# A gated mLSTM and mixture-of-experts block on one core: expert tiles written out, routing counts in a bank of their own, and warm-up matmuls in the routing waits

## What is computed

```python
def _L0_ffn_ref(hidden_states, w_gate, w1, w3, w2):
    E, TOPK, H, I = (8, 2, 256, 512)
    logits = SOFTCAP * jnp.tanh(x @ w_gate / SOFTCAP)      # 1024 tokens
    probs = jax.nn.softmax(logits, axis=-1)
    _, idx = jax.lax.top_k(probs, TOPK)
    weights = probs * one_hot(idx, E).sum(-2)
    for e in range(E):
        h = jax.nn.silu(x @ w1[e]) * (x @ w3[e])
        out = out + h @ w2[e] * weights[:, e:e + 1]
x = x + jnp.tanh(g_xattn[0]) * mlstm(_layernorm(x), ctx, ctx, ...)
x = x + jnp.tanh(g_ffn[0]) * _L0_ffn_ref(_layernorm(x), ...)
```

## Time and profile before

| | us |
|---|---|
| median of 3 runs | 223.19 (222.64 to 225.13) |
| profiled execution, its own time | 223.34 |
| its span, first to last instruction | 221.6 |

### The profile page before, as it was taken

The page is one execution under the profiler, slowest core; times in us unless marked ns, Lnnn a source line. Parts: engine busy times, 40 slices in busy tenths (PEclk is TensorE's granted clock), DMA queues, the critical chain, the costliest instruction groups (busy, mean ns, idle before and its releaser), DMA issues.

```text
span 221.6 us, 4536 instructions
## 1 busy us (share of the span) xinstructions
PE 194.2 (88%) x1327; PEld 139.9 (63%) x1328; DVE 159.6 (72%) x356; ACT 139.9 (63%) x281; POOL 92.1 (42%) x96
## 2 busy tenths in 40 slices
PE   8899899989889831779999999999999999999930
PEld 3378554444436621268888888888788888888720
DVE  6896764688989979998777857667666676767520
ACT  2487878898965697736666645565566665665510
POOL 8100254347470000611555556556445565642222
PEclk9999999999999885699999999999999999999997
DMA  4999999921010124120232233234333223343221
GB/s 111 313 366 376 372 374 373 372 77 47 3 47 3 57 77 151 47 53 24 47 50 47 47 50 49 47 49 70 50 55 59 51 47 47 47 57 37 27 24 24
DMA packets 20032, 23.41 MB, mean 106 GB/s; under 512 B 3888, under 2 KB 15152, under 8 KB 20016
## 3 DMA queue, kind: packets, MB, share of 16 engines
q1 hardware_dynamic: 13696, 16.94, 22.3%
q0 software_dynamic: 4464, 6.16, 17.2%
q10 hardware_dynamic: 1856, 0.10, 0.6%
HBM read 17.95 MB, written 5.24 MB: 105 GB/s over the span
## 4 chain that ended last, share of the span: by engine, by line
PE 72%; DVE 12%; ACT 5%; DMA 4%; issue 4%; POOL 1%; ACTq 0%; DVEq 0%; POOLq 0%
PE bank L1451 29%; PE bank L1266 7%; PE bank L1471 6%; PE bank L1483 5%; PE bank L1462 5%; PE bank L1306 3%; PE bank L1474 3%; DMA x_sb<-in_x_dram 3%; ACT arena L510 2%; PE bank L1433 2%; DMA out_dram<-hraw,sidx 2%; PE bank L1282 2%; PE bank L1337 1%; PE bank L1187 1%; DVE st L803 1%
## 5 line engine op out<-in xcount | busy, mean ns | idle before, releaser
L470 POOL DMA_INDIRECT out_dram<-hraw,sidx x23 | 37.6, 1633 | 52.5 <-DVE hraw L1140 32.8
L1451 PE MATMUL bank<-arena_r,xn_sb_r 128*128 x184 | 57.1, 391 | 0.0
L1451 PE MATMUL bank<-w_sb_r,xn_sb_r 128*128 x92 | 38.2, 415 | 1.5 <-DVE xn_sb_r L1084 1.2
L1451 PEld LDWEIGHTS bank<-arena_r,xn_sb_r 128*128 128x128 f32 x184 | 34.6, 188 | 7.0
L431 POOL TENSOR_SCALAR_AFFINE_SELECT arena<-arena 128x1024 f32<-128x1024 f32 x16 | 17.6, 1102 | 36.6 <-ACT arena L540 36.6
L674 ACT ACTIVATE x_sb<-bank 128x512 f32<-128x512 f32 x23 | 13.8, 599 | 28.6 <-PE bank L1451 28.6
L453 POOL DMA_INDIRECT cvT<-xnorm_scratch,gidx x12 | 13.8, 1146 | 32.1 <-DVE gidx L1038 24.2
L853 DVE TENSOR_TENSOR arena<-bank,arena 128x1024 f32<-128x1024 f32 x16 | 19.6, 1222 | 6.7 <-POOL arena L431 6.6
L1089 DVE TENSOR_TENSOR x_sb<-x_sb,bank 128x512 f32<-128x512 f32 x23 | 15.7, 684 | 9.0 <-ACT x_sb L674 8.9
L1451 PEld LDWEIGHTS bank<-w_sb_r,xn_sb_r 128*128 128x128 f32 x92 | 17.3, 188 | 5.0 <-issue 2.2
L975 DVE TENSOR_TENSOR w_sb_r<-w_sb,arena_r 128x512 fp32r<-128x512 f32 (+1 forms) x32 | 20.1, 684 | 0.1
(11 more groups left out here) (229 smaller groups left out, 389.6 us busy)
## 6 DMA issues: line engine op xcount, KB each, us to landing
w_sb<-in_L_ffn_w_dram SPq DMA_DIRECT2D x24, 512.0 KB, 9.2
x_sb<-in_x_dram SPq DMA_DIRECT2D x2, 512.0 KB, 6.7
arena<-in_ctx_dram SPq DMA_DIRECT2D x2, 512.0 KB, 9.4
out_dram<-x_sb SPq DMA_DIRECT2D x8, 128.0 KB, 1.8
xnorm_scratch<-xn_sb SPq DMA_DIRECT2D x8, 128.0 KB, 1.7
out_dram<-hraw,sidx POOLq DMA_INDIRECT x23, 3.8
cvT<-xnorm_scratch,gidx POOLq DMA_INDIRECT x12
hraw<-xnorm_scratch,gidx POOLq DMA_INDIRECT x11, 3.3
```

The costliest lines, as they stand in the source:

```text
L470: nc.gpsimd.indirect_dma_start(out=out[:, :], out_offset=bass.IndirectOffsetOnAxis(ap=sidx[:, i:i + 1], axis=0), in_=y_sb[i % 2], in_offse ...
L1451: last = nc.tensor.matmul(ps_scores[p][:, n, :], a, w, start=(k == 0 and j == 0), stop=(k == KC - 1 and j == 2))
```

## The change

- **Loops written out.** The `Fori` loops of ACT and DVE over the expert tiles become plain Python loops, with constant semaphore values and offsets. PE's loop stays. On DVE the load of a tile's expert moves from the start of a step to between `lower_w2` and `hidden` of the step before.
- **A third y buffer.** `y_sb` gets `zrow` as a third entry, and the wait on earlier scatters is one tile looser.
- **Counts.** PE makes the counts ahead of the ranks, in `ps_tr`, with a signal of their own (`s_cnt`); one more matmul with a constant adds 63.5. DVE rounds them up to whole tiles by a max and an add of 2^30 in float32, and the scan takes 2^30 off again, so `starts` holds slots. `ctile` and the reduction over it go.
- **slotf** is copied by ACT.
- **lower_weights(0, 2)** moves from before the wait for the ranks to behind `tabc`, beside parts 1 and 3.
- **Warm-ups.** 16 behind the last logits, 14 behind the ranks, 1 between the two groups of table matmuls, 15 for 8 behind the tables, 4 behind `turn_x(0)`.
- **The first gate-up** takes its 12 matmuls in another order: the 8 with the upper part of x first, waiting for `s_xh`; then the 4 with the lower part, waiting for `s_xts`.

```diff
@@ ACT
             act.wait_ge(s_slf, 1)
+            follow(nc.scalar.activation(slotf[:], sloti[:, 1, NS - LATE_OH:], ACT.Copy))
...
-            with act.Fori(1, E // 2) as pair:
...
+            for e in range(2, E):
+                for k in range(SPLIT):
+                    upper_weights(e, k)
+                store_hT(e - 2, e % 2)
+                silu(e - 1, (e - 1) % 2)
+                upper_x(e, e % 2)
...
-            with act.Fori(FAST, NT - 2, 2) as i:
...
+            for i in range(FAST, NT - 2):
+                upper_hT(i, i % 2)
+                upper_w2(i + 1, 1 - i % 2)
+                silu(i + 1, 1 - i % 2)
+                upper_x(i + 2, i % 2)
+                second_part(i)
@@ DVE, routing
-            lower_weights(0, 2)
+            dve.wait_ge(s_cnt, 1)
+            link(nc.vector.tensor_scalar(ntile[:, 1:], ps_tr[:, 0:E], P // 2 + 0.5, ROUND, ALU.max, ALU.add))
+            link(nc.vector.tensor_tensor_scan(starts[:], ntile[:], unround[:], 0.0, ALU.add, ALU.add))
+            base, eslot = starts[:, 0:E], starts[:, 1:]
+
             dve.wait_ge(s_rank, 1)
-            link(nc.vector.tensor_tensor(ctile[:], ps_small[:, 192:192 + E].unsqueeze(2).to_broadcast([P, E, E]),
-                                         iota_c[:, :].unsqueeze(1).to_broadcast([P, E, E]), ALU.is_gt))
-            link(nc.vector.tensor_reduce(ntile[:, 1:], ctile[:], AX_X, ALU.add))
-            link(nc.vector.tensor_tensor_scan(starts[:], ntile[:], zeros[:], 0.0, ALU.add, ALU.add))
...
+            link(nc.vector.tensor_tensor(slotm[:], base.unsqueeze(1).to_broadcast([P, B, E]),
+                                         ps_small[:, 128:128 + B * E].rearrange("p (b e) -> p b e", b=B), ALU.add))
...
-            nc.vector.tensor_scalar(sloti[:, 1, :], sloti[:, 0, :], P - 1, None, ALU.bitwise_and).then_inc(s_vch, 1)
-            chain[0] += 1
+            nc.vector.tensor_scalar(sloti[:, 1, :], sloti[:, 0, :], P - 1, None, ALU.bitwise_and).then_inc(s_slf, 1)
             link(nc.vector.tensor_scalar(sloti[:, 2, :], sloti[:, 0, :], 7, None, ALU.logical_shift_right))
-            nc.vector.tensor_copy(slotf[:], sloti[:, 1, NS - LATE_OH:]).then_inc(s_slf, 1)
...
-            lower_weights(0, 1)
-            lower_weights(0, 3)
+            for k in range(1, SPLIT):
+                lower_weights(0, k)
@@ DVE, tiles
-            def sum_y(i, p):
+            def sum_y(i):
                 dve.wait_ge(s_yp, i - FAST + 1)
-                dve.wait_ge(s_add, 16 * i - 16)
+                dve.wait_ge(s_add, 16 * (i - YBUF + 1))
...
-            with dve.Fori(2, E // 2) as pair:
...
+            for e in range(4, E):
+                split(e)
+                hidden(e - 1, (e - 1) % 2)
+                lower_x(e, e % 2)
+                scale_y(e - 2)
...
-            with dve.Fori(FAST, NT - 2, 2) as i:
...
+            for i in range(FAST, NT - 1):
+                lower_hT(i, i % 2)
+                lower_w2(i + 1, 1 - i % 2, e)
+                if i + 2 < NT:
+                    e = expert_of(i + 2)
+                hidden(i + 1, 1 - i % 2)
+                if i + 2 < NT:
+                    lower_x(i + 2, i % 2)
+                sum_y(i)
@@ PE
             logits(3)
+            warm_up(16)
             pe.wait_ge(s_mask, 1)
+            for i in range(B):
+                nc.tensor.matmul(ps_tr[:, 0:E], ones_b[:], mk[:, i * E:(i + 1) * E], start=(i == 0), stop=False)
+            nc.tensor.matmul(ps_tr[:, 0:E], ones_b[:], half_b[:], start=False, stop=True).then_inc(s_cnt, 1)
...
-            for i in range(B):
-                last = nc.tensor.matmul(ps_small[:, 192:192 + E], ones_b[:], mk[:, i * E:(i + 1) * E],
-                                        start=(i == 0), stop=(i == B - 1), skip_group_check=True)
             last.then_inc(s_rank, 1)
+            warm_up(14)
             for n in range(NS):
+                if n == SOME[1]:
+                    warm_up(1)
...
             last.then_inc(s_tab, 1)
-            warm_up(8)
+            warm_up(15)
...
+            def first_gate_up():
+                e = expert_of(0)
+                pe.wait_ge(s_wl, SPLIT)
+                pe.wait_ge(s_xh, 1)
+                for lower in range(2):
+                    if not lower:
+                        parts = ((xhT_sb[0], w13_r), (xhT_sb[0], arena_r))
+                    else:
+                        pe.wait_ge(s_xts, 1)
+                        parts = ((xlT_sb[0], arena_r),)
...
             turn_x(0, s_xg[0], 16, 0)
-            gate_up(0, 0, expert_of(0), 0)
+            warm_up(4)
+            first_gate_up()
```

More of the change, by code:

```diff
@@ L64, in bass_gated_mlstm_moe_kernel @@
     GATHER = 4
+    YBUF = 3
     SPLIT = W13 // I
@@ L1089, in hidden, with scale_y @@
                 nc.vector.tensor_tensor(h_sb[p], sg_sb[p], ps_scores[p][:, 1, :], ALU.mult).then_inc(s_hm, 1)
[L1091 removed]
+            def scale_y(i):
                 dve.wait_ge(s_y, i + 1)
[L1093 to L1095 removed]
+                if i >= YBUF:
+                    dve.wait_ge(s_add, 16 * (i - YBUF + 1))
+                nc.vector.tensor_scalar(y_sb[i % YBUF], ps_tr[:, 0:H], wslot[:, bass.ds(i, 1)], None,
                                         ALU.mult).then_inc(s_ys, 1)
@@ L1111, in _ @@
             lower_x(3, 1)
-            scale_y(1, 1, True)
-            with dve.Fori(2, E // 2) as pair:
-                for p in range(2):
-                    e = 2 * pair + p
-                    split(e)
-                    hidden(e - 1, 1 - p)
-                    lower_x(e, p)
-                    scale_y(e - 2, p)
+            scale_y(1)
+            for e in range(4, E):
[3 more added lines that the diff above has]
+                scale_y(e - 2)
             def expert_of(i):
@@ L1135, in lower_w2 @@
                                             half[:, :, 0, :].bitcast(F32), ALU.subtract).then_inc(s_wdl, 1)
-            def sum_y(i, p):
+            def sum_y(i):
                 dve.wait_ge(s_yp, i - FAST + 1)
-                dve.wait_ge(s_add, 16 * i - 16)
-                nc.vector.scalar_tensor_tensor(out=y_sb[p], in0=ps_tr[:, 0:H], scalar=wslot[:, bass.ds(i, 1)],
+                dve.wait_ge(s_add, 16 * (i - YBUF + 1))
+                nc.vector.scalar_tensor_tensor(out=y_sb[i % YBUF], in0=ps_tr[:, 0:H], scalar=wslot[:, bass.ds(i, 1)],
                                                in1=y_part, op0=ALU.mult, op1=ALU.add).then_inc(s_ys, 1)
             dve.wait_ge(s_eti, 1)
-            lower_w2(FAST, 1, expert_of(FAST))
+            e = expert_of(FAST)
+            lower_w2(FAST, 1, e)
+            e = expert_of(FAST + 1)
             hidden(FAST, 1)
             lower_x(E, 0)
-            scale_y(FAST - 1, 0)
-            with dve.Fori(FAST, NT - 2, 2) as i:
-                for n in range(2):
-                    p = 1 - n
-                    e = expert_of(i + n + 1)
-                    lower_hT(i + n, p)
-                    lower_w2(i + n + 1, 1 - p, e)
-                    hidden(i + n + 1, 1 - p)
-                    lower_x(i + n + 2, p)
-                    sum_y(i + n, p)
-            e = expert_of(NT - 1)
-            lower_hT(NT - 2, 1)
-            lower_w2(NT - 1, 0, e)
-            hidden(NT - 1, 0)
-            sum_y(NT - 2, 1)
+            scale_y(FAST - 1)
+            for i in range(FAST, NT - 1):
[7 more added lines that the diff above has]
+                sum_y(i)
             lower_hT(NT - 1, 0)
-            sum_y(NT - 1, 0)
+            sum_y(NT - 1)
         @block.tensor
@@ L1503, in tile_step @@
                     down(i - 1, 1 - p, e_before)
+            def first_gate_up():
[8 more added lines that the diff above has]
+                        parts = ((xlT_sb[0], arena_r),)
+                    for n in range(2):
+                        for k in range(KC):
+                            for j, (a, w) in enumerate(parts):
+                                last = nc.tensor.matmul(ps_scores[0][:, n, :], a[:, k * P:(k + 1) * P],
+                                                        w[:, bass.ds(e * W13 + (n * KC + k) * I, I)],
+                                                        start=(not lower and k == 0 and j == 0),
+                                                        stop=(lower == 1 and k == KC - 1), skip_group_check=True)
+                last.then_inc(s_gu, 1)
             turn_x(0, s_xg[0], 16, 0)
-            gate_up(0, 0, expert_of(0), 0)
+            warm_up(4)
+            first_gate_up()
             turn_x(1, s_xg[1], 16, 1, 1)
```

57 lines of the change are left out of this document (19 added, 38 removed).

## The result

The changed kernel takes 222.11 us (median of 20 runs, 221.11 to 224.78) and the kernel before 223.27 (20 runs, 222.46 to 225.56); the ratio is 0.9946, with an interval of 0.992 to 0.9973. Half a per cent faster, well inside the 1% that was called "within"; 222.1 had been forecast. The ratios leave out runs more than 1.5% above the shortest of their kernel (2 of these 20) while the medians are over all runs, and the 8 runs of the changed kernel above 223 us show a mean granted clock of 0.979 to 0.986, the other 12 one of 0.986 to 0.994.

What follows compares the result with a forecast made beforehand. DVE's queue, tied with PE's path, was taken to bound the routing, and PE the tiles. From 223.34 us, -0.2 (routing) and -1.0 (tiles) gave 222.1 us; own range 221.5 to 222.8, runs' spread included 221.0 to 223.6.

Steps and rivals of the forecast that it cites:

- within: Whole kernel: the measured time lies less than 1% from the kernel before, 221.0 to 225.4 us; chance 0.80.
- What bounds each stage: Routing: PE's gather path and DVE's queue tie at `hidden(0)`; tiles 1 to 6 and 7 to 22: PE.
- the small routing term: Routing up to `hidden(0)`: DVE stays 0.2 us ahead, so -0.2 us, bounds 0 to 0.4.
- The steps up to `gidx`: Routing on DVE: earlier counts gain 0.7 us, `slotf` on ACT about 0.1; `gidx` at about 88.8, not 89.62.
- The split that returns: DVE behind `gidx`: the moved `lower_weights(0, 2)` comes back as a third L975 of 0.60 us, leaving 0.2 gained.
- the tie at `hidden(0)`: Before `hidden(0)`: silu and `split(1)` end together; after the change DVE comes last, the silu a full microsecond earlier.
- The tile term: Tiles from `turn_h(7)` to `turn_h(21)`: loops written out bring 4.94 to 4.87 us each, 14 x 0.07 = 1.0 us.
- The load in front of hidden: DVE in the late tiles: the expert's load takes at most 0.41 us and stays hidden, 0.38 to spare.
- the third buffer: Scatters of y: costed at nothing, since a scatter needs 4.7 us, less than the 4.87 of a tile.
- The warm-ups: PE's idle time in the routing: 42 more matmuls, all hidden at full clock; the clock they keep up buys little.
- The rival in which the clock falls among the 16: Routing warm-ups: clock falls at 82.2, all of DVE behind `s_tab` 3.4 us late, total 225.5; chance 0.07.
- The order of the first gate-up: First gate-up on PE: no longer waiting for `lower_x` saves about 0.5 us, but with DVE last it gives nothing.

Runs made afterwards that it cites:

- hidden first: The changed kernel with hidden(0) and lower_x(1) on DVE taken ahead of the last part of split(1); 221.34 us, ratio 0.9901 to the kernel before.
- the load moved: The changed kernel with DVE's load of the expert back at the head of a tile, loops still written out; 221.98 us, ratio 0.9911 to the kernel before.

## Why the prediction was right, and where its steps were off

- **What bounds each stage** held, with one correction. PE sets tiles 1 to 6 (`turn_h(0)` to `turn_h(7)`: 36.61 before, 36.58 after) and the tiles from 7 on. DVE's queue sets the first hidden value of the changed kernel; moving the split back, which changed `gidx` by 0.42 and the first hidden value by nothing, confirms the step on which the small routing term rested. In the kernel before it is the silu that comes last, by 0.15: the value starts 2.56 us after the start of the four L975 (95.78) and not 2.41. But that path, too, hangs on DVE, since the old gate-up waits for `lower_x`.
- **The routing term was too small**: -0.2 forecast, with bounds of 0 and 0.4, and -0.65 measured. The steps up to `gidx` were right: mask to `slotm` shortened by 0.72 (0.7 forecast), mask to `gidx` by 0.91 (0.8). The 0.1 beyond the forecast fits the clock: tables at half clock were taken to end ahead of DVE, and without the warm-ups `gidx` comes 0.13 later. The split that returns took its 0.6, which leaves 0.31 at the reduction L1045, where 0.2 was forecast. More was missed behind it. One small DVE operation, L1052 of before, took 0.41 us there and 0.23 as L1047 here, which is 0.18. And the tie at `hidden(0)` was costed at nothing; the silu's 0.15 went as well. The small operation in the timeline of before, with POOL's second gather:

```profile
91.46 1.33 POOL L453 DMA_INDIRECT cvT<-xnorm_scratch,gidx  x1 [0.30 <-issue]
...
92.36 0.41 DVE L1052 TENSOR_SCALAR r<-r,tg 128x8 f32<-128x8 f32 x1
```

In the four profiles in which it takes 0.41 (before, the loops alone twice, the split moved back) it starts during that gather and ends 0.02 us before it. In the ten in which it takes 0.23 it starts 0.17 or 0.18 us after the gather's end. So it looks as if POOL's instruction held it, and as if the split, now ahead of it, moved it out of the way; no run tests that.
- **The tile term was too large**: -1.0 forecast, -0.65 measured in every kernel with the loops written out. Two steps failed. The forecast took the first tile, 4.86, as the floor of all. Only that one and the last three or so come down to it; the others take 4.89 to 4.92, which is the early tile of the earlier trace rows, where PE was busy 4.90 of 4.90. And it divided a total evenly rather than look at each late tile. In the timeline of before, later on:

```profile
155.44 0.65 PE L1462 MATMUL bank<-ident,x_sb 128*128 128x128 f32 x4
...
160.51 0.65 PE L1462 MATMUL bank<-ident,x_sb 128*128 128x128 f32 x4
...
165.42 0.65 PE L1462 MATMUL bank<-ident,x_sb 128*128 128x128 f32 x4
...
170.40 0.65 PE L1462 MATMUL bank<-ident,x_sb 128*128 128x128 f32 x4
```

The late tile from 155.44 is 5.07 long, that from 165.42 only 4.98. The six late tiles are 5.07, 5.07, 4.98, 4.99, 4.98 and 4.94; over 4.90 that makes 0.63, nearly all that was gained. Why the later ones stall less stays open.
- **The load in front of hidden** was rightly costed at nothing, and so was the third buffer: the experiments on each show 68.55, the changed kernel 68.53.
- **The warm-ups** were costed at nothing while the clock stays up; by the marks they give 0.24 at `turn_h(7)` (52.09 against 52.33), which no time shows. The rival in which the clock falls among the 16 was in no profile: what happened was falls some 6 us earlier, which cost 1.6 in one execution (76.5) and 0.15 to 0.2 in two others. The rival had 3.4, because it let the clock stay down through the 14; in all three it was back before they began.
- **The order of the first gate-up** was costed at nothing because DVE comes last; it is worth the 0.15 by which the silu would come last without it.
- **The sum.** Two errors of opposite sign, -0.45 in the routing and +0.35 in the tiles, nearly cancel: -1.3 by the marks and -1.16 by the medians, -1.2 forecast. That the total came so near is luck in good part; what was read rightly is which engine comes last in each stage after the change. The profiled execution, 221.37, lies 0.74 under the median, and its mask came 0.71 early.

Open: what makes the clock fall in one execution of a kernel and not in the next. Each kernel was profiled in one execution only (the changed one and the loops alone in two), so where the clock fell in the other runs is not known.

## What to carry to other kernels

Where two paths tie, count the whole queue of the engine that comes last: an operation moved within that queue gives next to nothing, and one moved behind the consumer gives its length until the other path comes last (0.61 us here, a whole part of the split, with 0.15 to spare). Before a stall is multiplied by the number of tiles, read each of its tiles, and take as the floor the tile in which the bound engine was already full. Filler work goes only where the work behind it in the same queue can bear its slow case: in these profiles a clock that fell where the engine mostly waits cost 0.1 to 0.3 us, and one that fell where the chain runs through the engine cost 1.6.

## What the runs showed of the hardware

- The granted clock fell at different places in different executions of like code, among these: at 75.4 before, at 75.2 to 75.7 with hidden first, without the new warm-ups and with two buffers, at 76.5 with the load moved, in the first gate-up with the loops alone (not in that kernel's second profile), in the second gate-up with two buffers, and nowhere up to the last matmul in the changed kernel's two profiles. In the windows of 0.5 us in which these falls lie PE was busy 0.46 us or more. In the five profiles without the new warm-ups (before, the loops alone twice, and the two kernels without them) it also fell between 80.8 and 82.2, where PE had waited since 78.6 to 79.7.
- A load of a register ahead of a gate-up costs PE's stream 0.45 us (0.88 against 0.43).
- A small DVE operation took 0.41 us in place of 0.23 whenever it started during POOL's second gather (4 of 14 profiles); the cause is not shown.
- Writing out the loops cost almost no fetching of instructions: the DMA queue q14 carried 6 packets and 0.05 MB before, and this after:

```profile
q14 instruction: 8, 0.07, 0.1%
```

The Trainium skill, "Runtime: NRT & Kernel Launch", Instruction fetch mechanics, says that straight code is streamed at little cost and that a taken branch to code outside the pages held stalls for a fetch. This case agrees with the first: two packets more, and tiles that are no longer. Of the second it shows nothing: with the loops the queue carried fewer packets, so nothing here puts the turn's 0.59 us down to a fetch.
